# A graph layer's feature sums: ScalarE copies them out, and three accumulating products turn them in the bank rotation

## The reference

```python
src_h = h[src] @ W_msg.T + b_msg
emb = edge_embed[jnp.clip(edge_type, 0, NUM_EDGE_TYPES)]
msg = src_h + emb
messages = jax.ops.segment_sum(msg, dst, num_segments=num_nodes)
h_new = _gru_cell(messages, h[:num_nodes], W_ih, W_hh, b_ih, b_hh)
...
x = _layernorm(x + h_new)
```

## Time and profile before

| | us |
|---|---|
| median of 3 runs | 1253.09 (1248.27 to 1254.03) |
| profiled execution, device time | 1256.97 |
| profiled execution, span of the trace | 1255.1 |
| PE busy in the span | 1037.9 (83%) |
| DVE busy | 859.2 (68%) |
| ACT busy | 660.5 (53%) |
| mean granted TensorE clock | 0.926 of full |

### The profile page before, as it was taken

How to read it: one execution, slowest core, us unless ns; L and a number is a source line. 1 busy time by engine, 2 the same in 40 slices (tenths; PEclk the granted TensorE clock), 3 DMA queues, 4 the chain that set the end, 5 groups by cost and what they waited for, 6 DMA issues and landing times.

```text
span 1255.1 us, 23526 instructions
## 1 busy us (share of the span) xinstructions
PE 1037.9 (83%) x8411; PEld 656.5 (52%) x8411; DVE 859.2 (68%) x2699; ACT 660.5 (53%) x1283; POOL 733.5 (58%) x779
## 2 busy tenths in 40 slices
PE   5456677888888988989889989889888888888884
PEld 2124354555555555556556656555555555555552
DVE  8413557677776877868777767777876777676644
ACT  4243404455655555656666656555655556554622
POOL 7725645665566666666666666566666666566640
PEclk9566568999999999999999999999998999999996
DMA  8529311222222322322333223223323233332321
GB/s 244 159 79 310 107 33 53 78 77 74 74 77 79 91 77 77 91 78 77 82 83 92 79 78 92 74 79 92 90 77 89 76 89 83 86 92 80 83 81 28
DMA packets 94565, 114.23 MB, mean 91 GB/s; under 512 B 19820, under 2 KB 80616, under 8 KB 94441
## 3 DMA queue, kind: packets, MB, share of 16 engines
q0 software_dynamic: 35264, 73.19, 21.8%
q1 hardware_dynamic: 57320, 37.79, 10.2%
q10 hardware_dynamic: 1856, 1.66, 0.5%
HBM read 96.56 MB, written 16.00 MB: 90 GB/s over the span
## 4 chain that ended last, share of the span: by engine, by line
PE 64%; issue 10%; DVE 9%; ACT 7%; another core or an unknown queue 7%; DMA 1%; SPq 1%; DVEq 0%; ACTq 0%
PE psf L1097 28%; PE psb L1082 14%; PE pAB L1026 5%; PE psg L1065 4%; PE pAB L1040 4%; ACT mem L1213 3%; DVE ohl L868 2%; PE pAB L1043 2%; DVE ohk L862 2%; PE psg L1069 2%; PE psf L1102 1%; DMA arena<-in_x 1%; ACT mem L1153 1%; DVE ohk L865 1%
## 5 line engine op out<-in xcount | busy, mean ns | idle before, releaser
L604 POOL DMA_INDIRECT xg<-x_split,idx x648 | 616.1, 951 | 392.1 <-PE psg L1069 151.0
L1213 ACT CAST mem<-psb 128x432 f16<-128x432 f32 x896 | 426.7, 525 | 398.4 <-PE psb L1082 300.8
L1097 PE MATMUL psf<-mem 128*128 128x384 bf16 (+1 forms) x2744 | 618.4, 330 | 13.6 <-issue 6.8
L1082 PE MATMUL psb<-ohk,ohl 128*128 128x108 bf16 (+3 forms) x1865 | 421.6, 264 | 97.9 <-issue 57.4
L862 DVE TENSOR_TENSOR ohk<-table_bank,prm 128x392 bf16<-128x392 f16 (+3 forms) x437 | 271.0, 620 | 108.6 <-PE psb L1082 69.1
L1097 PEld LDWEIGHTS psf<-mem 128*128 128x128 f16 (+1 forms) x2744 | 240.4, 99 | 131.3 <-issue 34.9
L1082 PEld LDWEIGHTS psb<-ohk,ohl 128*128 128x128 bf16 x1865 | 173.6, 100 | 251.3 <-issue 116.4
L868 DVE TENSOR_TENSOR ohl<-table_bank,prm 128x512 bf16<-128x512 f16 x437 | 180.8, 414 | 0.0
L891 DVE TENSOR_TENSOR mem<-mem,psg 128x136 f32 (+9 forms) x184 | 54.9, 298 | 168.4 <-remote 106.8
L604 POOL DMA_INDIRECT xg<-in_x,idx x88 | 84.2, 957 | 76.3 <-PE psg L1069 44.7
L865 DVE TENSOR_TENSOR ohk<-table_bank,sort 128x40 bf16<-128x40 f16 (+3 forms) x437 | 106.5, 244 | 0.0
(11 more groups left out here) (148 smaller groups left out, 808.4 us busy)
## 6 DMA issues: line engine op xcount, KB each, us to landing
xg<-x_split,idx POOLq DMA_INDIRECT x648
x_split<-mem SPq DMA_DIRECT2D x24, 384.0 KB
xb<-in_xT SPq DMA_DIRECT2D x49, 128.0 KB
arena<-in_x SPq DMA_DIRECT2D x24, 256.0 KB
arena<-in_xN SPq DMA_DIRECT2D x47, 128.0 KB
out<-spill SPq DMA_DIRECT2D x19, 128.0 KB
out<-arena SPq DMA_DIRECT2D x144, 8.0 KB
out<-arena SPq DMA_DIRECT2D x15, 128.0 KB
```

What stands on the lines that cost most here:

```text
L604: pool.indirect_dma_start(out=xg[:, p % RING, :] if split else xg32(p % RING), out_offset=None, in_=x_d if split else x, in_offset=bass.In ...
L1082: ins = pe.matmul(psb[:, bank % NB, held * HC:(held + m) * HC], ohl[:, e % KB, :], ohk[:, e % KB, d * HC:(d + m) * HC], start=(k == 0), st ...
L1097: pe.matmul(psf[:, 0:3 * H], Bb[q % 2][0:kk, HT + h, :], xs[0:kk, h, :, :].rearrange("p c f -> p (c f)"), start=(h == 0), stop=(h == HI - ...
L1213: act.copy(Bb[q % 2][:, :, n:n + MOST], psb[:, bank % NB, 0:MOST * HC].rearrange("p (d h) -> p h d", h=HC)).then_inc(S["s_eb"], 1)
```

## The change

S moves from DVE to ACT: one copy of `psf[:, 0:384]` to `parts` in SBUF, with no addition. T now makes three float32 products with the identity, one for each part, that accumulate in PSUM and so add and turn at once. T also makes the nine count products, which are no longer in the last F item. Both go to a bank of the `psb` rotation, so the rotation has 32 banks for a block's counts and one for its turn. C copies from that bank and signals `s_eb`, as the evictions do. The first F of the next block waits for the copy S (`s_sc`), no longer for C. The first eviction of a block waits for `s_tt` (T of two blocks before), no longer for `s_fd`, since the count products read `Bb` until then.

The planner's positions change too: S at 0.01, F from 0.06 on, and T and C together behind the first B item from position 0.10 on that closes a bank. `parts` shares its bytes with an index table that is copied to PSUM before.

```diff
-SETTLED = (0.02, 0.06, 0.10)
-CLEAR = 0.17
+SUMMED = 0.01
+TURNED = 0.10
+CLEAR = 0.06
...
+CLOSED = frozenset(e for e in range(SLOTS_N) if BANK_LAST[pieces(e)[-1][0]] == e)
...
-                       [(at, u) for at, (_, u) in zip(SETTLED, late)])
+                       [(SUMMED, u) for _, u in late[:1]])
+        if late:
+            k = next(k for k, (at, u) in enumerate(mixed) if at >= TURNED and (not own or u[0] == "B" and u[1] in CLOSED))
+            mixed[k + 1:k + 1] = [(mixed[k][0], u) for _, u in late[1:]]
...
+def rotation():
+    banks, turns, evicted = {}, {}, []
+    for it in ITEMS:
+        if it[0] == "B":
+            for b, _, _, _ in pieces(it[1]):
+                banks.setdefault(b, len(banks) + len(turns))
+            evicted += [banks[b] for b, _, _, _ in pieces(it[1]) if BANK_LAST[b] == it[1]]
+        elif it[0] == "T":
+            turns[it[1]] = len(banks) + len(turns)
+        elif it[0] == "C":
+            evicted.append(turns[it[1]])
+    assert evicted == list(range(BANKS + NQ))
+    return banks, turns
+
+
+BANK_AT, TURN_AT_BANK = rotation()
...
-                    elif it[0] == "S":
-                        q = it[1]
-                        v.wait_ge(S["s_fd"], q + 1)
-                        if q:
-                            v.wait_ge(S["s_tt"], q)
-                        v.tensor_reduce(added[:, :], psf[:, 0:3 * H].rearrange("p (c f) -> p f c", c=3), AX, ALU.add
-                                        ).then_inc(S["s_sc"], 1)
...
                     elif b < CB0:
-                        pe.wait_ge(S["s_cp"], 2 * b + 2)
+                        pe.wait_ge(S["s_eb"], TURN_AT_BANK[2 * b + 1] + 1)
...
-                            if bank >= NB and held == 0 and k == 0:
-                                pe.wait_ge(S["s_eb"], bank - NB + 1)
-                            ins = pe.matmul(psb[:, bank % NB, held * HC:(held + m) * HC], ohl[:, e % KB, :],
+                            at = BANK_AT[bank]
+                            if at >= NB and held == 0 and k == 0:
+                                pe.wait_ge(S["s_eb"], at - NB + 1)
+                            ins = pe.matmul(psb[:, at % NB, held * HC:(held + m) * HC], ohl[:, e % KB, :],
...
                         if f == 0:
-                            pe.wait_ge(S["s_eb"], (q + 1) * FB // MOST)
+                            pe.wait_ge(S["s_eb"], BANK_AT[(q + 1) * FB // MOST - 1] + 1)
...
-                                pe.wait_ge(S["s_cp"], q)
+                                pe.wait_ge(S["s_sc"], q)
...
                     elif it[0] == "T":
                         q = it[1]
+                        at = TURN_AT_BANK[q]
                         pe.wait_ge(S["s_sc"], q + 1)
-                        pe.matmul(psf[:, 0:FB], added[:, :], ident[:, :], start=True, stop=True, skip_group_check=True
-                                  ).then_inc(S["s_tt"], 1)
+                        pe.wait_ge(S["s_eb"], at - NB + 1)
+                        for c in range(3):
+                            pe.matmul(psb[:, at % NB, 0:FB], parts[:, c * H:(c + 1) * H], ident[:, :], start=(c == 0),
+                                      stop=(c == 2), skip_group_check=True)
+                        for t in range(NT):
+                            ins = pe.matmul(psb[:, at % NB, FB:2 * FB], sel[:, NT - 1 - t:NT - 1 - t + P], Bb[q % 2][:, t, :],
+                                            start=False, stop=(t == NT - 1), skip_group_check=True)
+                        ins.then_inc(S["s_tt"], 1)
...
                             if q >= 2 and n == 0:
-                                act.wait_ge(S["s_fd"], q - 1)
+                                act.wait_ge(S["s_tt"], q - 1)
...
+                    elif it[0] == "S":
+                        q = it[1]
+                        act.wait_ge(S["s_fd"], q + 1)
+                        if q:
+                            act.wait_ge(S["s_tt"], q)
+                        act.copy(parts[:, :], psf[:, 0:3 * H]).then_inc(S["s_sc"], 1)
...
-                        act.copy(cnts[0:ND2, 0, o:o + FB], psf[0:ND2, 3 * H:3 * H + FB])
-                        act.copy(den[:, o:o + FB], psf[:, 0:FB]).then_inc(S["s_cp"], 1)
+                        at = TURN_AT_BANK[q] % NB
+                        act.copy(cnts[0:ND2, 0, o:o + FB], psb[0:ND2, at, FB:2 * FB])
+                        act.copy(den[:, o:o + FB], psb[:, at, 0:FB]).then_inc(S["s_eb"], 1)
```

More of the change, by code:

```diff
@@ L366, in gnn_kernel @@
         flag = sb("flag", [1, 1], I32)
-        iota = sb("iota", [P, MOST * HC], F16)
+        parts = sb("parts", [P, 3 * H])
+        iota = parts[:, 0:MOST * HC // 2].bitcast(F16)
         ident = sb("ident", [P, P])
@@ L385, in gnn_kernel @@
         sel = sb("sel", [P, NT - 1 + P], BF16)
-        added = sb("added", [P, H])
         tohs = sb("tohs", [P, ND2])
@@ L447, in gnn_kernel @@
         names = ("s_idx s_gl s_dt s_tl s_lb s_w s_io s_id s_d s_mg s_sg s_bg s_fl s_tab s_dc s_so "
-                 "s_blk s_ptr s_z s_bad s_sum s_prm s_tm s_te s_cp s_si s_st "
+                 "s_blk s_ptr s_z s_bad s_sum s_prm s_tm s_te s_si s_st "
                  "s_bi s_em s_cn s_used s_oh s_acc s_ok s_kd s_eb s_fd s_toh s_tr s_sl s_main "
@@ L942, in _ @@
                                         slow_typ[:, bass.ds(t, 1)].unsqueeze(2).to_broadcast([P, 2, NT]),
-                                        iota[:, 0:NT].unsqueeze(1).to_broadcast([P, 2, NT]),
+                                        count_up[:, 0:NT].unsqueeze(1).to_broadcast([P, 2, NT]),
                                         ALU.is_equal).then_inc(S["s_toh"], 1)
@@ L1018, in final @@
                     if second(i, slow) and not gone(i, slow):
-                        pe.wait_ge(S["s_eb"], BANKS)
+                        pe.wait_ge(S["s_eb"], BANKS + NQ)
                     elif i:
@@ L1093, in _ @@
                             else:
-                                pe.wait_ge(S["s_cp"], q)
+                                pe.wait_ge(S["s_sc"], q)
                         for h in range(HI * f // PARTS, HI * (f + 1) // PARTS):
                             kk = P if h < HI - 1 else TAIL
-                            pe.matmul(psf[:, 0:3 * H], Bb[q % 2][0:kk, HT + h, :],
-                                      xs[0:kk, h, :, :].rearrange("p c f -> p (c f)"),
-                                      start=(h == 0), stop=(h == HI - 1), skip_group_check=True)
+                            ins = pe.matmul(psf[:, 0:3 * H], Bb[q % 2][0:kk, HT + h, :],
+                                            xs[0:kk, h, :, :].rearrange("p c f -> p (c f)"),
+                                            start=(h == 0), stop=(h == HI - 1), skip_group_check=True)
                         if f == PARTS - 1:
-                            for t in range(NT):
-                                ins = pe.matmul(psf[:, 3 * H:3 * H + FB], sel[:, NT - 1 - t:NT - 1 - t + P], Bb[q % 2][:, t, :], start=False,
-                                                stop=(t == NT - 1), skip_group_check=True)
                             ins.then_inc(S["s_fd"], 1)
@@ L1211, in _ @@
                             if q >= 2 and n == 0:
-                                act.wait_ge(S["s_fd"], q - 1)
+                                act.wait_ge(S["s_tt"], q - 1)
                             act.copy(Bb[q % 2][:, :, n:n + MOST],
-                                     psb[:, bank % NB, 0:MOST * HC].rearrange("p (d h) -> p h d", h=HC)
+                                     psb[:, BANK_AT[bank] % NB, 0:MOST * HC].rearrange("p (d h) -> p h d", h=HC)
                                      ).then_inc(S["s_eb"], 1)
+                    elif it[0] == "S":
[4 more added lines that the diff above has]
+                        act.copy(parts[:, :], psf[:, 0:3 * H]).then_inc(S["s_sc"], 1)
                     elif it[0] == "C":
```

## The result

| | kernel before | changed kernel |
|---|---|---|
| median, us (4 runs each, side by side) | 1253.56 | 1269.06 |
| ratio, 95% interval | | 1.0116 [1.0069, 1.0163] |
| profiled execution, device time / span, us | 1256.97 / 1255.1 | 1272.63 / 1270.7 |
| PE / DVE / ACT busy, us | 1037.9 / 859.2 / 660.5 | 1042.1 / 847.0 / 666.4 |

What follows compares the result with a forecast made beforehand. PE was taken as the bound, with holes worst in the handoffs between blocks. The terms -16 + 10 + 11 - 4 - 9 gave -8 us, 1249 against the profiled 1256.97, so 1245 us against the median; range 1231 to 1266.

Steps and rivals of the forecast that it cites:

- term 1: Handoff from a block's last F to the next first F: PE's holes shrink from 46 to 30 us, -16 us.
- term 2: T on PE: six float32 passes for two, 0.35 us more in each of 28 turns, +10 us.
- term 3: B item behind T: PE waits for the gated first eviction, 0.57 us in 19 periods, +11 us (bounds 0 and +23).
- term 4: Half-clock stretches of the dense part: shorter handoff holes save half of four of them, -4 us.
- term 5: DVE without the reduction: one-hots come earlier for PE's B items, a third of 28 us gained, -9 us.
- A: Rival, chance 0.20: B items behind T wait 1.3 us for busy ACT, +15 us, 1268; decides from 0.84 us on.
- B: Rival, chance 0.29: holes move to PE's later waits for one-hots and evictions, half the gains absorbed, about -3 us, 1250.

Runs made afterwards that it cites:

- r4: Changed kernel with the nine count products back in the last F and the first eviction not gated by T; slower kind of chip, 0.9979 of the kernel before.
- e5: Changed kernel with the count products back in the last F and one float32 product in T for three; slower kind, 0.9977 of the kernel before.
- e7: Changed kernel with the count products first inside T, signalling the gated eviction before the three float32 products; slower kind, 0.9966 of the kernel before.
- e6: Changed kernel with count products back in the last F, the sum on DVE and one product in T; slower kind, 0.9974 of the kernel before.
- r5: The same kernel as e6, run again on another chip of the slower kind; 1.0001 of the kernel before.
- r7: The changed kernel itself, unaltered, run on a chip of the faster kind; 1.0222 of the kernel before.

## Why the prediction was wrong, point by point

The terms against the two profiled executions. Of 28 turns 27 lie in the dense part.

| | forecast | measured |
|---|---|---|
| term 1, handoff | -16 | -18.5 (holes 53.9 to 35.4) |
| term 2, added passes | +10 | +11.6 (12.0 x 27/28) |
| term 3, gated eviction | +11 | +29.3 (27.1 before the ninth B product in 18 blocks, 2.2 in the nineteenth) |
| term 4, clock | -4 | -1, within the next |
| term 5, DVE | -9 | -4.2 (other holes 131.6 to 127.4) |
| before and behind the dense part | 0 | +1.1 and -3.6 |
| sum | -8 | +15.6 (spans 1255.1 to 1270.7) |

**Term 1 was right.** The next block starts as said: F0 comes 2.30 us after the last F (62.17 over 27) where 1.9 was forecast, with 1.3 us of hole where 1.1 was. The holes of before were somewhat longer than the 46 us read from the records. The copy took what was interpolated for it, 0.48 us:

```profile
L1244 ACT COPY parts<-psf x28: 459/488/538, 224.1 to 1234.0; 128x384 f32<-128x384 f32 x28
```

These are the shortest, the median and the longest in ns. The Trainium skill's estimate in "ScalarE: Activation LUTs", section "Rules for kernel authors", would have been 0.62; the measurement decides against it.

**Term 2 was right in size**: six passes start 0.73 us before the count products (816.45 to 817.18) where 0.67 was forecast. That all of it is paid was right in the sum of the stream, but on this kind of chip taking them away again, with the gate gone, gave nothing that shows (`r4`, `e5`).

**Term 3 is the step that failed.** The list of its pieces was 0.22 for the product, 0.05 to wake ACT, 0.525, 0.15. The first two together are the turn's signal, priced at 0.27. Measured are 1.22 us in the median of all turns and up to 3.3, and the hole is 1.54 us for each of 19 blocks (29.3) and not 0.57. On the faster kind, where the signal comes at 0.23, it is 0.50 (9.4): the mechanism and the arithmetic were right, and the duration taken for "product done" was not. It was taken from the length of a record, where a signal of the same engine behind as long a run of short products, the sparse group's, would have given 1.4. With that the hole would have been 0.57 - 0.27 + 1.37 = 1.67 us, the term 32 us, and the sum +13 for -8: slower. The upper bound of 23 us let ACT be late, but never PE's signal. `e7`, which removes most of the term, and `r4`, which removes all of it, give back 16 to 20 and 14 to 18 us of the dense part. That is half to three quarters of what the hole measured. In `r4`, against the three traces of the changed kernel, 5 to 6 us came back in the handoffs and 6 to 10 in the other holes.

**Term 4 didn't come.** The dense part has eight stretches at half clock before, one of them twice as long, and eight of 3.4 us after: one length less, worth 1.7 us at most and 0.7 by the columns that ran in them. The two other traces of the changed kernel have nine and ten, so nothing was saved. One of the eight now begins at 822.3, right behind the hole of 3.5 us in the turn shown above. Holes were moved, not removed.

**Term 5 came by half at most.** DVE is busy for 12.2 us less, but PE's other holes shrank by 4. The 45 us of the earlier trace rows from which it was argued, moreover, are those of the whole dense part, and not only outside the handoffs. `e6` and `r5` say it from the other side: DVE busy for 17 us more, and the time the same.

**The rivals.** A gave 1268, and that is the time that came; its place (the B products behind the turn) and about its size (25 us) are right too, and so is its point of decision, 0.84 us a block, with 1.54 measured. Its reason is not: it had ACT late, with evictions, copies and table loads in a row, and ACT sat idle for 6.2 us. That its time came out is luck to that extent. B was half right, since more than half of two expected gains (terms 4 and 5) was absorbed. But PE's waits at B for DVE's one-hots fell, from 8.9 to 3.7 us. Those for evictions grew from 14.5 to 25.0, and those whose releaser the profile doesn't show from 45.0 to 65.8: 26 us for the three together, about the hole at the ninth B product. A chance of 0.20 was too small for a wait that was new, on the bounding engine's path, and priced with the lengths of records and not with a signal.

## What to carry to other kernels

When a change adds a wait for PE, price the signal from pairs of PE and waiter in the trace that had nothing else to wait for, best behind as many short products as the new one has, and not from the length of the last product's record. When a step both reads a buffer that others want back and does more, let it read first and signal there, and do the rest behind it: the same products in another order were worth 16 to 20 us of the dense part on one kind of chip here and 8.6 on the other. And a trade between engines measured on one chip holds for its kind: where PE is busy for 91% of the span, passes added to it counted nearly in full, and where it is busy for 83%, with the gate gone, not so that it showed.

## What was not expected of the hardware

The chips fell into two kinds, on which the same kernel before takes 1254 and 1084 us, at busy times of PE in the changed kernel of 1042 and 999 us and granted clocks of 0.934 and 0.972. On the faster kind the change costs 2.2% where it costs 1.0 to 1.2% on the slower, and counts first, the best version on the slower kind with a gain of 0.3%, loses 1.2% on the faster. On the slower kind PE's signals come late, 0.9 to 1.2 us in the median and up to 3.3 behind 15 short products, and on the faster one the turn's never later than 0.44 us. The kinds differ in more than the signals: before the dense part the changed kernel takes 223 us on the slower kind and 155 on the faster, and of these the clock is at half for 130 and 48 us. In the dense part it is at half for 27 to 34 us on the slower kind and in `r7` never. What makes the chips differ, and whether the late signals are the cause of the 170 us between them or another effect of it, stays open.
